# Moving mixed tiles and exponentials out of units 2 to 4 of a chained FFN block

## The reference, cut to what matters

```python
# _bi_wkv(r=x, k=v=fside): per channel, forward and backward scan over time
ek, ekv = exp(k), exp(k) * v
a = a * decay + ekv_t ; b = b * decay + ek_t        # both directions
base = sigmoid(r) * (num / den)
mix  = base * (0.8 + 0.2 * tf)
# FFN on the mix, 1024 -> 4096 -> 1024
h = einsum('bsd,fd->bsf', mix, W1)
a = gelu(clip(round(h / 0.1)) * 0.1)
out = x + einsum('bsf,df->bsd', a, W2)
```

## Time and profile before

| what | value |
|---|---|
| median of three runs | 1805.2 us |
| the profiled execution | 1801.47 us, span 1799.2 us, mean granted clock 0.983 |
| TensorE busy | 1665.2 us, 93% of the span |
| VectorE busy | 1292.5 us, 72% |
| ScalarE busy | 972.4 us, 54% |
| DMA, 16 engines | 210 GB/s on average |

### The profile page before, as it was taken

One profiled execution on the slowest core, in us unless ns is written; L12 is line 12 of the kernel. 1 busy time (PEld: TensorE's weight loads), 2 busy tenths in 40 slices (PEclk: granted clock), 3 DMA queues, 4 the chain that ended last, 5 costly groups with the idle time before them and its releaser, 6 DMA issues. The chain is left out here.

```text
span 1799.2 us, 30815 instructions
## 1 busy us (share of the span) xinstructions
PE 1665.2 (93%) x12258; PEld 1202.8 (67%) x12258; DVE 1292.5 (72%) x1787; ACT 972.4 (54%) x1480; POOL 24.6 (1%) x44
## 2 busy tenths in 40 slices
PE   1579999899999999989999999989999999999998
PEld 0134444778648885678856887478865888578874
DVE  8976867697597966789586975969769795755222
ACT  4367532674637736486555846377364764555140
POOL 0000020000000000000000000000000000000000
PEclk9789999999999999999999999999999999999999
DMA  9858795658475774657746585656847577465744
GB/s 240 208 148 251 271 323 186 214 178 276 162 244 178 235 246 141 223 175 253 247 144 222 186 270 168 234 170 202 275 132 265 168 245 232 146 216 181 237 146 142
DMA packets 153461, 376.97 MB, mean 210 GB/s; under 512 B 15328, under 2 KB 44256, under 8 KB 152800
## 3 DMA queue, kind: packets, MB, share of 16 engines
q1 hardware_dynamic: 150624, 351.86, 58.8%
q0 software_dynamic: 2688, 23.07, 5.6%
HBM read 347.61 MB, written 67.11 MB: 231 GB/s over the span
## 5 line engine op out<-in xcount | busy, mean ns | idle before, releaser
L748 PE MATMUL ps<-mo,w_ring 128*128 128x256 f16 x6272 | 707.3, 274 | 52.8 <-DVE q L1610 22.5
L748 PEld LDWEIGHTS ps<-mo,w_ring 128*128 128x128 f16 x6272 | 615.0, 98 | 140.6 <-issue 56.2
L891 PE MATMUL ps<-act,w_ring 128*128 128x512 f16 x1760 | 383.3, 379 | 0.0
L811 PE MATMUL ps<-act,w_ring 128*128 128x256 f16 x3136 | 348.6, 273 | 1.0 <-DVE act L1673 1.0
L811 PEld LDWEIGHTS ps<-act,w_ring 128*128 128x128 f16 x3136 | 306.1, 98 | 37.7 <-DVE act L1673 1.8
L891 PEld LDWEIGHTS ps<-act,w_ring 128*128 128x128 f16 x1760 | 172.2, 98 | 203.2
L1642 DVE SCALAR_TENSOR_TENSOR act<-a,act 128x1024 f16<-128x1024 f32 x72 | 88.0, 1223 | 156.5 <-ACT act L1152 156.5
L1177 ACT ACTIVATE q<-tt 128x1024 int8<-128x1024 f32 x64 | 67.2, 1050 | 203.8 <-DMA tt<-in_w_dram 203.7
L1142 ACT ACTIVATE a<-q 128x1024 f32<-128x1024 int16 x128 | 135.3, 1057 | 14.9 <-DVE act L1642 10.7
L1705 DVE SCALAR_TENSOR_TENSOR tt<-q,tt 128x1024 f32<-128x1024 int8 x64 | 78.1, 1221 | 71.1 <-ACT q L1177 71.1
L877 PE MATMUL ps<-act,w_ring 128*128 128x512 f16 x512 | 110.8, 379 | 3.1 <-DVE xy L1686 3.1
(11 more groups left out here) (121 smaller groups left out, 1694.1 us busy)
## 6 DMA issues: line engine op xcount, KB each, us to landing
w_ring<-w1s SPq DMA_DIRECT2D x168, 512.0 KB, 4.3
w_ring<-w_half SPq DMA_DIRECT2D x130, 512.0 KB, 4.8
tt<-in_w_dram SPq DMA_DIRECT2D x64, 512.0 KB, 5.3
w_ring<-w2s SPq DMA_DIRECT2D x56, 512.0 KB, 4.7
V<-in_fside_dram SPq DMA_DIRECT2D x64, 256.0 KB, 5.3
R<-in_x_dram SPq DMA_DIRECT2D x64, 256.0 KB, 5.3
w_half<-in_w_dram POOLq DMA_DIRECT2D x16, 1024.0 KB, 8.5
xy<-in_x_dram SPq DMA_DIRECT2D x64, 256.0 KB, 5.4
```

Source lines behind the costliest of these rows:

```text
L748: mm = pe.matmul(dst[:, f, :], wp_ring[:, k, r, f, q, :], mo[:, op, q, p, :], start=(fresh and f == 0 and q == 0 and p == 0), stop=(q == K ...
L811: mm = pe.matmul(dst[:, i, :], wy_ring[:, k, i, 2 * s + j, :], ao[:, s, op, j, p, :], start=(fresh and i == 0 and s == 0 and j == 0 and p ...
L891: mm = pe.matmul(bank[d][:, :], w2_ring[:, k, FPS * (s - SPLIT) + j, :], act[:, act_at(n, s) + j, p, :], start=(s == SPLIT and j == 0 and ...
```

## The change

The first tile of the next block stays where it was. Tile 1's group on ACT goes into unit 1, ahead of the first gelu and without a table load. On DVE units 2, 3 and 4 get one quarter each (tile 1's first three) instead of two, and `quantise22` is put ahead of it. The rest goes behind unit 4: tiles 2 to 4 into the partial outputs, tiles 4 and 5 into units 5 to 7. Four of the checks, not three, now stand ahead of `quantise11` of unit 5. SP's tile loads move with them. ACT has six groups with a table load instead of seven, and tile 4 and 1 without one.

```diff
@@ ffn_block, SP
-                    if nxt and s in (2, 4):
-                        load_tile(g0 + s // 2 + 1)
+                    if nxt and s == 2:
+                        load_tile(g0 + 2)
...
                 load_check(at)
+                if nxt:
+                    load_tile(g0 + 3)
                 ring_load()
-                if nxt:
-                    load_tile(g0 + 4)
                 store_quad(n, 0, 0)
                 ring_load(3)
                 load_quad(n, 1, 0)
                 load_check(at + 1)
                 ring_load(2)
+                if nxt:
+                    load_tile(g0 + 4)
                 store_quad(n, 0, 3)
                 store_quad(n, 0, 1)
                 ring_load(2)
-                if nxt:
-                    load_tile(g0 + 5)
+                load_check(at + 2)
                 store_quad(n, 0, 2)
...
                 load_quad(n, 1, 2)
-                load_check(at + 2)
-                ring_load(3)
-                if nxt:
-                    load_tile(g0 + 6)
-                ring_load()
+                ring_load(2)
+                if nxt:
+                    load_tile(g0 + 5)
+                load_check(at + 3)
+                ring_load(1)
                 store_quad(n, 1, 3)
                 store_quad(n, 1, 1)
-                ring_load()
+                ring_load(2)
                 store_quad(n, 1, 2)
-                load_check(at + 3)
                 ring_load(2)
+                if nxt:
+                    load_tile(g0 + 6)
                 ring_load(4)
-                if nxt:
-                    load_tile(g0 + 7)
                 residual(n, 0)
                 residual(n, 1)
                 load_check(at + 4)
+                if nxt:
+                    load_tile(g0 + 7)
@@ quantise11, ACT
                 if s == SPLIT + 1:
-                    act_e.wait_ge(s_chk, DT * n + 3)
+                    act_e.wait_ge(s_chk, DT * n + 4)
@@ check_i8, ACT: at % DT < 3 becomes at % DT < 4
@@ chained_block, ACT
                 quantise11(n, 0)
+                seed(hid(n, 1))
+                spill_p5(hid(n, 1))
+                quantise12(n, 0)
+                if nxt:
+                    tile_group(g0 + 1)
+                gelu(n, 0, 0)
+                quantise11(n, 1)
+                quads_hi_11(n, 0)
...
-                    if nxt and s in (2, 4):
-                        tile_group_between(g0 + s // 2)
...
                 spill_p5(part_y(n, 0))
                 if nxt:
-                    tile_group_between(g0 + 3)
+                    tile_group_between(g0 + 2)
...
                 spill_p5(part_y(n, 1))
                 if nxt:
-                    tile_group_between(g0 + 4)
+                    tile_group_between(g0 + 3)
                 check_i8(at + 1)
                 seed(hid(n, SPLIT + 1))
                 spill_p5(hid(n, SPLIT + 1))
+                if nxt:
+                    tile_group(g0 + 4)
                 check_i8(at + 2)
-                if nxt:
-                    tile_group(g0 + 5)
+                check_i8(at + 3)
                 quantise11(n, SPLIT + 1)
...
                 act_hi(n, SPLIT + 1, 1)
+                if nxt:
+                    tile_group_between(g0 + 5)
                 spill_p5(hid(n, LAST))
...
                     operands_hi(n + 1, 0)
-                check_i8(at + 3)
+                check_i8(at + 4)
                 if nxt:
                     tile_group_between(g0 + 7)
                     operands_hi(n + 1, 1)
-                check_i8(at + 4)
                 check_i8(at + 5)
@@ chained_block, DVE, s = 2 to 4
                     quads_lo_2(n, s - 2)
-                    mix(s // 2, 0 if s % 2 == 0 else 2)
                     quantise22(n, s - 1)
                     quads_lo_t(n, s - 2, 0)
                     quads_lo_t(n, s - 2, 1)
-                    mix(s // 2, 1 if s % 2 == 0 else 3)
+                    mix(1, s - 2)
                     seed_u4(hid(n, s))
...
                 quantise22(n, SPLIT)
-                mix(2, 2)
-                act_lo(n, SPLIT, 0)
-                mix(2, 3)
-                seed_u4(part_y(n, 0))
-                mix(3, 0)
-                y11(n, 0)
-                mix(3, 1)
-                act_lo(n, SPLIT, 1)
-                mix(3, 2)
-                check(at)
-                y22(n, 0)
-                mix(3, 3)
+                mix(1, 3)
+                act_lo(n, SPLIT, 0)
+                mix(2, 0)
+                seed_u4(part_y(n, 0))
+                y11(n, 0)
+                mix(2, 1)
+                act_lo(n, SPLIT, 1)
+                mix(2, 2)
+                check(at)
+                mix(2, 3)
+                y22(n, 0)
                 y12(n, 0)
-                mix(4, 0, 1)
+                mix(3, 0, 1)
                 check(at + 1)
                 y11(n, 1)
                 seed_u4(part_y(n, 1))
+                mix(3, 2)
                 y21(n, 0)
-                mix(4, 2, 3)
+                mix(3, 3)
                 y22(n, 1)
                 check(at + 2)
                 y12(n, 1)
-                mix(5, 0)
+                mix(4, 0, 1)
                 seed_u4(hid(n, SPLIT + 1))
+                check(at + 3)
+                mix(4, 2)
                 y21(n, 1)
-                mix(5, 1)
                 quantise22(n, SPLIT + 1)
+                mix(4, 3)
                 act_lo(n, SPLIT + 1, 0)
-                mix(5, 2)
                 seed_u4(hid(n, SPLIT + 2))
+                mix(5, 0, 1)
                 act_lo(n, SPLIT + 1, 1)
-                mix(5, 3)
                 quantise22(n, SPLIT + 2)
+                mix(5, 2)
                 act_lo(n, SPLIT + 2, 0)
                 seed_u4(hid(n, LAST))
+                mix(5, 3)
...
                 mix(6, 1)
-                check(at + 3)
+                check(at + 4)
...
                 mix(7, 1)
-                check(at + 4)
+                check(at + 5)
                 residual_sum(n, 3)
                 mix(7, 2, 3)
-                check(at + 5)
```

More of the change, by code:

```diff
@@ L605, in ffn_block @@
                 load_quad(n, 1, 2)
-                load_check(at + 2)
-                ring_load(3)
+                ring_load(2)
[3 more added lines that the diff above has]
+                ring_load(1)
+                store_quad(n, 1, 3)
+                store_quad(n, 1, 1)
+                ring_load(2)
+                store_quad(n, 1, 2)
+                ring_load(2)
                 if nxt:
                     load_tile(g0 + 6)
-                ring_load()
-                store_quad(n, 1, 3)
-                store_quad(n, 1, 1)
-                ring_load()
-                store_quad(n, 1, 2)
-                load_check(at + 3)
-                ring_load(2)
                 ring_load(4)
-                if nxt:
-                    load_tile(g0 + 7)
                 residual(n, 0)
@@ L1173, in check_i8 @@
                 act_e.wait_ge(s_chkload, 16 * (at + 1))
-                act_e.wait_ge(s_gelu, half_of(n, SPLIT - 1 if n > 0 and at % DT < 3 else LAST, 1) + 1)
+                act_e.wait_ge(s_gelu, half_of(n, SPLIT - 1 if n > 0 and at % DT < 4 else LAST, 1) + 1)
                 if at > 0:
@@ L1210, in chained_block @@
                 quantise11(n, 0)
[L1211 to L1214, removed]
+                seed(hid(n, 1))
[6 more added lines that the diff above has]
+                quads_hi_11(n, 0)
+                for s in range(2, SPLIT + 1):
+                    quantise21(n, s - 2)
+                    gelu(n, s - 2, 1)
                     seed(hid(n, s))
-                    if s >= 2:
-                        quads_hi_2(n, s - 2)
+                    quads_hi_2(n, s - 2)
                     spill_p5(hid(n, s))
-                    if s >= 2:
-                        quads_hi_t(n, s - 2)
-                    if nxt and s in (2, 4):
-                        tile_group_between(g0 + s // 2)
+                    quads_hi_t(n, s - 2)
                     quantise12(n, s - 1)
@@ L1833, in chained_block @@
                 y12(n, 1)
-                mix(5, 0)
+                mix(4, 0, 1)
                 seed_u4(hid(n, SPLIT + 1))
+                check(at + 3)
+                mix(4, 2)
                 y21(n, 1)
-                mix(5, 1)
                 quantise22(n, SPLIT + 1)
+                mix(4, 3)
                 act_lo(n, SPLIT + 1, 0)
+                seed_u4(hid(n, SPLIT + 2))
+                mix(5, 0, 1)
+                act_lo(n, SPLIT + 1, 1)
+                quantise22(n, SPLIT + 2)
                 mix(5, 2)
-                seed_u4(hid(n, SPLIT + 2))
-                act_lo(n, SPLIT + 1, 1)
-                mix(5, 3)
-                quantise22(n, SPLIT + 2)
                 act_lo(n, SPLIT + 2, 0)
                 seed_u4(hid(n, LAST))
+                mix(5, 3)
                 act_lo(n, SPLIT + 2, 1)
```

## The result

The changed kernel takes 1822.5 us (median of four runs, 1817.3 to 1825.4) against 1804.8 us for the one before (four runs, 1799.8 to 1807.4). The ratio is 1.0098, with an interval of 1.0064 to 1.0132: slower by about 1%, where 1783.8 us, a gain of 1.2%, had been forecast. The profiled execution took 1820.21 us, 18.7 us more than that of before.

What follows compares the result with a forecast made beforehand. The prediction took TensorE's waits on DVE and ACT work (52.8 us) as what could be regained: 37.4 removed - 21.0 new cost + 5 at block ends = 21.4 us, 1780.1 profiled, 1783.8 us as median; range 1769 to 1797.

Steps and rivals of the forecast that it cites:

- The fourth check: Start of unit 6: the check's load and the work behind it make late blocks lose 1.0 us, even ones 0.4.
- What is removed: TensorE's waits in units 1 to 4, for unit 6's seed_u4 and at L811 go: 37.4 us gained.
- The tight place: Unit 2 of a late block: quantise22 done at 775.5, needed at 775.9, fits by 0.3 us, costed at nothing.
- What moves to the partial outputs: Quarters and tile loads moved into the partial outputs are covered by idle stretches there and cost nothing.
- Tile 5 ahead of unit 6's fourth quadrant: Unit 6: that quadrant waits 3.3 us in late blocks, 0.4 in even, plus 1.7 us of slower clock in late ones.
- The end of a block: One check fewer behind unit 7 shortens waits at the next block's start: 5 us gained in all, ends 0 and 8.
- (c): Rival: slower, the check's landing bounds unit 6's start; gain gone at a landing of 9.6 us, 1811 at 10.6; chance 0.05.
- (a): Rival: tile 5 costs little, the clock stays and unit 6's wait is half; 1769 to 1775 us; chance 0.2.
- (d): Rival: units 2 to 4 hang on ACT, so 15 of the 37.4 us stay as waits; 1798 us; chance 0.07.
- (b): Rival: thin covers, unit 2 misses, check lands 1 to 2 us later, block ends give nothing; 1790 to 1796; chance 0.18.

Runs made afterwards that it cites:

- The edit on the kernel before: Kernel before, with only quantise22 put ahead of the unit's first quarter on DVE in units 2 to 4, no quarter moved: 1798.2 us, ratio 0.9965.
- mended_three: Kernel after, fourth check back in its old place, y21 ahead of mix(4, 2), unit 6's quantise22 and unit 7's seed_u4 ahead of tile 5's quarters: 1771.4 us.
- y21_first: Kernel after, with y21 of the second partial output ahead of the fourth check and mix(4, 2) on DVE: 1788.3 us, ratio 0.9907.

## Why the prediction was wrong

**The step that failed is "The fourth check"**, and in it one consumer. I followed what stands behind the check on DVE, `mix(4, 2)`, `y21` and `quantise22` of unit 5, and asked only when the last of them is needed. That was nearly right: I had it ready at T + 11.5, with T = 872.98 the start of unit 6, and its row ends at 885.25, T + 12.3. Who waits for `y21` I didn't ask. It is `seed` of unit 6, through the bank, and TensorE needs it at T + 6.98; it came 5.5 us late (5.34 idle and 0.16). In place of 1.0 us in late and 0.4 in even blocks this term measured 5.5 us on average for the wait alone (33.0 / 6), and about 45 us in six blocks with latency and clock, where I had 4.2. The kernel with `y21` in front shows it to be this: what the term covered is left there, 9.9 us in six blocks, and the time is 1788.3, within 5 us of the forecast.

**Its other part was also too small.** With `y21` out of the way, late blocks lose 1.7 to 2.6 us and even ones 1.2 to 1.3. I had taken 6.0 us for the landing from rows with 3.9 to 10.6; it measured 6.6 in block 3 and 7.0 on average, and the load was issued at T - 1.5 in block 3, not T - 2.0. The terms that I named also add up to T + 7.4 and T + 11.2, 0.2 to 0.3 us less than the T + 7.6 and T + 11.5 that I wrote.

**"What is removed" held**: 37.4 us were named and are gone from the groups. The tight place, `quantise22` in unit 2 of a late block, was in time: TensorE has 416 matmuls without a gap there. The edit on the kernel before adds that the order alone gives 7 us of it; the rest needs the quarters moved.

**"What moves to the partial outputs" held**: L813 shows 0.0 idle.

**"Tile 5 ahead of unit 6's fourth quadrant" held to 0.15 us**: 3.43 measured in late blocks for 3.3, 0.51 in even ones for 0.4. For the clock I took 1.7 us per late block; the three calls of 16 lost 1.6 each. The other outcome, a drain of 1380 ns in every switch of tables as the Trainium skill has it ("ScalarE: Activation LUTs", "What ACT_TABLE_LOAD costs"), would have made this wait 1.4 us longer. These rows from the kernel after, ACT and DVE of tile 5 in block 3, don't show it:

```profile
895.55 1.28 ACT L1062 ACT_TABLE_LOAD   x1
896.84 0.63 ACT L1023 ACTIVATE EKP<-VP 128x512 f32<-128x512 f32 x1
...
898.80 0.69 DVE L1432 SCALAR_TENSOR_TENSOR EE<-EKP,EE 128x512 f32<-128x512 f32 x1 [6.65 <-ACT EE L1031]
```

The first exponential starts 1.29 us after the load does, and the weight is there 3.25 us after it, the same as in the earlier trace rows.

**"The end of a block" held**: 5.2 us of waits for 5, and 1.5 us of slow matmuls besides. With the fourth check put back the waits are there again, 7.7 us idle against 5.9 before the change, so the check's place is what counts here.

**Rivals.** (c) had the sign, the place (the start of unit 6, behind the fourth check on ACT) and roughly the time (1811), but not the cause: I asked for a landing of 9.6 us, and 7.0 was enough, since `y21` stood behind the landing, the check and a quarter. (a) and (d) didn't occur. Of (b) one part did, the check landing 1 us later; the prices in (b) add up to 14 to 18 us, so that its time should have been 1798 to 1802 and not 1790 to 1796. The chance of 0.05 rested on the landing's median alone. What I had not counted was a chance that a consumer was missing from my walk, and a change that reorders so many steps in three queues deserves one.

## What to carry to other kernels

When a step moves on an in-order queue, list, for each step that now comes behind it, all who wait for that step, also those that wait for its buffer to come free; the last step of the chain may be in time and one in the middle 5 us late. Put a step that waits for a DMA behind all that the bounding engine, here TensorE, needs soon, above all when little waits for the step itself: here `y21` behind the check and not ahead of it cost 34 us, and the place of the check's load was worth 27 us or 2 us depending on what stood behind it. And price a wait of 5 us with the matmuls after it, which cost a further 1.3 to 2.8 us each time in these runs.

## What the runs showed of the hardware

Behind the same wait of 2.72 us the clock sometimes falls and sometimes doesn't. In block 3 it fell in the kernel before (176 matmuls in 21.02 us), in `mended_three` and in two more kernels (47.2 and 46.9 us for 416); it stayed in the kernel after, where the 416 matmuls from 766.43 took 45.57 us at full rate, and in seven more kernels. In block 5, with the same wait, it fell in seven of the twelve kernels, four of which had kept it in block 3; `y21_first` took 45.57 us in the one block and 47.24 in the other. From the windows view, first `mended_three` around its wait before 747.78:

```profile
720.00:740.00 20.00, 20.00 (x120) 11.51 (x119) 15.77 (x26) 9.39 (x13) 0.00 (x0) 1.00 0.87 311
740.00:760.00 20.00, 17.28 (x144) 14.61 (x142) 11.18 (x16) 11.36 (x25) 0.00 (x0) 0.91 0.48 149
```

and the kernel after around its wait before 766.43:

```profile
760.00:780.00 20.00, 17.28 (x159) 15.26 (x158) 11.18 (x16) 13.01 (x26) 0.00 (x0) 1.00 0.54 166
```

The granted clock is 0.91 in the one and 1.00 in the other, with the same idle time; it is 1.00 in the stretch before the first, too. What decides it these runs don't show. Behind waits of 3.4 us and more slow matmuls followed every time in unit 6: 0.5 to 1.7 us lost over 16 matmuls, 1.3 to 2.2 over 144, up to 2.8 over 160. The loss can hardly be forecast wait by wait, but in the kernel after its sum was over a third of the waits themselves (17.5 of 44.8 us).
